# Feed-forward first pass: the stores of normed and transposed rows move from SyncE's queue to ScalarE's

## The reference, cut to what matters

```python
# x: (2, 2048, 1024) float32, N = 4096 rows, D = 1024
x = _layernorm(x + attention(x))            # 32 heads, causal; then out @ wo
# feed-forward, on rows xf = x.reshape(4096, 1024)
h = relu(layernorm(xf @ gw1.T + gb1) * ln_gamma + ln_beta)   # 32 wide
gates = h @ gw2.T + gb2                                       # 8 experts, top 2
counts = onehot.sum(axis=0); allowed = counts <= capacity     # over ALL rows
main = xf @ weight.T
tmp  = einsum('ni,eir->enr', xf, lora_A) * w.T[:, :, None]
out  = main + einsum('enr,ero->no', tmp, lora_B) / 16
x = _layernorm(x + out)
```

## Time and profile before

| | |
|---|---|
| median of 3 runs | 3506.47 us (3506.14 to 3508.07) |
| the profiled execution | 3506.97 us, of which the span is 3505.2 us |
| PE busy | 3426.8 us, 98% of the span |
| DVE / ACT / POOL busy | 2013.6 / 1459.9 / 1743.8 us (57% / 42% / 50%) |
| DMA queues for data | one (q1), 247904 packets, 336.87 MB, 32.2% of 16 engines' span |
| stretch of the first pass | about 2600 to 3110 us |

### The profile page before, as it was taken

The page is one execution under the profiler, slowest core; times in us unless marked ns, Lnnn a source line. Parts: engine busy times, 40 slices in busy tenths (PEclk is TensorE's granted clock), DMA queues, the critical chain, the costliest instruction groups (busy, mean ns, idle before and its releaser), DMA issues.

```text
span 3505.2 us, 61763 instructions
## 1 busy us (share of the span) xinstructions
PE 3426.8 (98%) x25202; PEld 2411.1 (69%) x25202; DVE 2013.6 (57%) x3618; ACT 1459.9 (42%) x1830; POOL 1743.8 (50%) x747
## 2 busy tenths in 40 slices
PE   8999998999999999999999999999998999999999
PEld 7888885566666666666665666666657888878887
DVE  3122116777777667677777767767655666642222
ACT  3111111555555555555555555555542332221111
POOL 0000002888988988898898898889550000000000
PEclk9999997999999999999999999999999999999999
DMA  6334325111121111112112111110037777654553
GB/s 214 114 123 120 113 90 127 26 51 48 32 54 50 35 42 50 42 34 51 48 32 54 50 31 47 50 38 11 26 106 217 234 234 234 211 201 173 173 173 130
DMA packets 248172, 340.60 MB, mean 97 GB/s; under 512 B 55520, under 2 KB 150240, under 8 KB 247904
## 3 DMA queue, kind: packets, MB, share of 16 engines
q1 hardware_dynamic: 247904, 336.87, 32.2%
HBM read 203.08 MB, written 133.17 MB: 96 GB/s over the span
## 4 chain that ended last, share of the span: by engine, by line
PE 78%; DVE 2%; ACT 2%; DMA 1%; issue 1%; POOL 0%; SPq 0%; ACTq 0%; POOLq 0%; DVEq 0%
PE p_o L682 19%; PE p_qm L647 17%; PE p_km L675 12%; PE p_acc L42 7%; PE p_acc L44 7%; PE p_acc L43 7%; PE p_km L668 3%; PE p_qm L651 2%; PE p_km L670 2%; ACT p_probs L759 2%; DVE p_part_max L795 1%; PE p_ag_ps L1096 1%; PE p_acc L1085 1%; DMA p_recip<-reciprocals 1%; PE p_ag_ps L1097 1%
## 5 line engine op out<-in xcount | busy, mean ns | idle before, releaser
L795 DVE TENSOR_REDUCE p_part_max<-p_qm 128x1 f32<-128x512 f32 (+3 forms) x2240 | 1407.0, 670 | 579.5 <-PE p_qm L647 328.8
L618 POOL TENSOR_TENSOR p_psums<-p_psums,p_probs 128x1024 f32<-128x1024 f32 x620 | 1479.3, 2386 | 93.3 <-ACT p_probs L755 2.8
L759 ACT ACTIVATE p_probs<-p_km 128x1024 f32<-128x1024 f32 x896 | 878.5, 1021 | 481.0 <-PE p_km L675 430.8
L647 PE MATMUL p_qm<-p_k_st,p_q_st 96*128 96x512 f32 (+3 forms) x2560 | 913.8, 421 | 12.4 <-DMA p_q_st<-q_hi 10.8
L647 PEld LDWEIGHTS p_qm<-p_k_st,p_q_st 96*128 96x128 f32 x2560 | 481.8, 195 | 254.2 <-issue 112.9
L675 PE MATMUL p_km<-p_q_st,p_k_st 97*128 97x512 f32 x1792 | 599.9, 417 | 13.5 <-ACT p_probs L759 8.7
L682 PE MATMUL p_o<-p_probs,p_v 128*32 128x256 f32 (+1 forms) x9216 | 565.5, 372 | 0.0
L682 PEld LDWEIGHTS p_o<-p_probs,p_v 128*32 128x32 f32 x9216 | 271.5, 110 | 216.7 <-issue 45.2
L675 PEld LDWEIGHTS p_km<-p_q_st,p_k_st 97*128 97x128 f32 x1792 | 312.1, 192 | 112.6 <-ACT p_probs L759 74.7
L614 POOL TENSOR_TENSOR p_psums<-p_probs 128x1024 f32<-128x1024 f32 x110 | 262.1, 2383 | 223.9 <-ACT p_probs L759 223.9
L33 POOL MEMSET p_ident<- 128x128 f32 x2 | 0.4, 204 | 551.0 <-POOLq L64 543.2
(11 more groups left out here) (153 smaller groups left out, 4004.0 us busy)
## 6 DMA issues: line engine op xcount, KB each, us to landing
p_q_st<-q_hi SPq DMA_DIRECT2D x128, 256.0 KB, 4.6
p_x_raw<-in_xT SPq DMA_DIRECT2D x64, 256.0 KB, 3.4
q_hi<-p_out_hi SPq DMA_DIRECT2D x64, 256.0 KB, 2.0
q_lo<-p_out_lo SPq DMA_DIRECT2D x64, 256.0 KB, 2.3
p_q_st<-q_lo SPq DMA_DIRECT2D x64, 256.0 KB, 4.3
attended_T<-p_o_raw SPq DMA_DIRECT2D x128, 128.0 KB
p_a_raw<-attended_T SPq DMA_DIRECT2D x32, 512.0 KB, 4.3
p_recip<-reciprocals SPq DMA_DIRECT2D x128, 128.0 KB, 6.6
```

Source lines behind the costliest of these rows:

```text
L618: pool.tensor_tensor(sums[:, :, :], sums[:, :, :], probs[(n * NS + s) % PB][:, :, :], ALU.add).then_inc(added, 1)
L647: last = pe.matmul(bank[:, x * keys:(x + 1) * keys], q_st[par][0:ROWS, c, h + x, sub * P:(sub + 1) * P], k_st[par][0:ROWS, j * CK:j * CK + ...
L759: act.activation(tile[:, :, :].rearrange("p h q -> p (h q)"), km[s % 2][:, :, :].rearrange("p a b -> p (a b)"), ACT.Exp, scale=SCALE).then ...
L795: dve.reduce_max(part_max[c][:, h:h + heads, sub, j], qm[bank_of(i)][:, 0:item_width(i)].rearrange("p (h k) -> p h k", h=heads), AX.X).the ...
```

## The change

The six lines that issue the three stores leave SP's step and become two functions on ACT, called at the end of ACT's step behind `split_a` and `hidden_root`, ahead of the weight's split. Every wait that stood ahead of a store on SP now stands ahead of it on ACT; SP's own waits for its loads are the same as before.

```diff
@@ sync @@
                     sp.wait_ge(sum_done, t)
                     load_x(t + 1)
-                if 2 <= t < NT + 2:
-                    u = t - 2
-                    sp.wait_ge(yT_lo_done, u + 1)
-                    sp.dma_start(yTh_d[u, :, :, :], yT_hi[:, :, :].bitcast(F32)).then_inc(yT_stored, 16)
-                    sp.dma_start(yTl_d[u, :, :, :], yT_lo[:, :, :].bitcast(F32)).then_inc(yT_stored, 16)
-                if 1 <= t <= NT:
-                    u = t - 1
-                    sp.wait_ge(y_done, u + 1)
-                    sp.dma_start(y_t[u, :, :], y[u % 2][:, :]).then_inc(y_stored[u % 2], 16)
                 if t + 2 < NT:
                     sp.wait_ge(a_lo_done, t + 2)
                     load_a(t + 2)
@@ scalar @@
+            def store_yT(u):
+                act.wait_ge(yT_lo_done, u + 1)
+                act.dma_start(yTh_d[u, :, :, :], yT_hi[:, :, :].bitcast(F32)).then_inc(yT_stored, 16)
+                act.dma_start(yTl_d[u, :, :, :], yT_lo[:, :, :].bitcast(F32)).then_inc(yT_stored, 16)
+
+            def store_y(u):
+                act.wait_ge(y_done, u + 1)
+                act.dma_start(y_t[u, :, :], y[u % 2][:, :]).then_inc(y_stored[u % 2], 16)
+
             def step(t):
@@ step @@
                 if 3 <= t < NT + 3:
                     hidden_root(t - 3)
+                if 2 <= t < NT + 2:
+                    store_yT(t - 2)
+                if 1 <= t <= NT:
+                    store_y(t - 1)
                 for n in range(KC):
                     if t == wm_step(n):
                         split_wm(n)
```

## The result

The changed kernel takes **3520.66 us**, median of 7 runs (3516.85 to 3522.46), against 3506.47 for the kernel before in 7 runs of its own (3505.66 to 3508.07). The ratio is 1.0038, interval 1.0027 to 1.0050: **14 us slower**. 3545.6 had been forecast. The profiled execution took 3519.35 us, with a span of 3517.6, 12.4 above the span before (3505.2).

The account below looks back on a forecast made before the run. PE's 14.6 us round bounds the kernel, the `a_raw` loop within 0.2 us of it. A 12.5 us load plus 3.6 makes 16.1 us; over 27 intervals +38.6 us on 3506.97 gives 3545.6 us, own range 3529 to 3581.

Parts of the forecast that it names:

- what binds: Steady first pass: PE fully busy at 14.6 us per round, the loop through `a_raw` at 14.4 us.
- T: The issue of a load of `a_raw`, at the end of `a_lo`; 3014.95 us in the step read.
- the assumed moment: Stores issued by ACT behind `hidden_root`, at T - 1.1, T - 0.7 and T - 0.3.
- The estimate by work: Load of `a_raw`: 4.0 us of store data less 1.1 us of lead adds 2.9 to 9.1, giving 12.0 us.
- the formula: Time added over the first pass's load loop: 27 P - 396.1, P the load interval; zero at 14.67 us.
- The size of the load at a given lead: Load of `a_raw` with the stores issued from T - 1.1: taken as 12.5 us, range 11.9 to 13.8.
- The base of 9.1 us: Length of the `a_raw` load before the change, read from load 28, issue to landing of the fourth reciprocal load.
- The estimate by landings: Load of `a_raw`: straight line between loads 7 and 4 by when `y` lands, giving 14.0 us.
- ACT's wait for `yT_stored` should stay away: Ahead of `yT_hi` on ACT: the second transposed store has 8.1 us to land, so the wait costs nothing.
- PE's waits of 1 to 2 us in most rounds: Expected sign at the hidden transpose on PE: waits of 1 to 2 us in most rounds.
- No change: Rival: stores fill half-idle DMA engines under the reciprocals, load stays under 11.1 us, 3507 us; chance 0.23.
- Faster: Rival at start-up: load 4 lands in 10.8 us or less, removing PE's stall, 7.7 us, 3499 us; chance 0.12.

Follow-up runs that it names:

- experiment 1: Changed kernel with the three stores still on ACT but ahead of `split_a` and `hidden_root`: 3504.56 us, ratio 0.9989 to the kernel before.
- experiment 4: Changed kernel with a second pair of `a_raw`/`recip` buffers for the odd tiles 3 to 21: 3501.40 us, ratio 0.9980 to the kernel before.
- experiment 5: Changed kernel with ACT waiting for the end of its own `split_a` before issuing the stores: 3554.38 us, ratio 1.0127 to the kernel before.
- experiment 3: Changed kernel with a second pair of `yT_hi`/`yT_lo` buffers for the odd tiles 3 to 19: 3522.03 us, ratio 1.0041 to the kernel before.
- experiment 9: Kernel before, stores on SP held back by a wait for `divide_a` to the moment the changed kernel issues them: 3518.59 us, ratio 1.0033.
- 7: Changed kernel with the edits of experiment 1 and experiment 4 together: 3500.77 us, ratio 0.9979 to the kernel before.
- six kernels of the table: Kernels before and after, experiment 1, experiment 5, experiment 9, and the kernel before with stores on SP behind the wait for `a_lo` (ratio 1.0215).

## Why the prediction was right and wrong

**Right: what binds.** PE had no slack in the steady part, and the loop through `a_raw` lay within 0.2 us of its round. Slower by over 0.2% had chance 0.65, and 3520.66 lies in 3504 to 3578, but below the forecast's own range (3529 to 3581). Experiment 1, which moves only the stores, takes the loss away, and so does experiment 4, which opens the loop.

**Wrong: "In the changed kernel ACT issues the stores behind `hidden_root`, which ends at 3013.87".** The order of the program says so, the chip does not. ACT's queue issued the stores at the start of `split_a` (2849.44 and 2849.44), not at its end. What fits the rows is that a DMA goes out as soon as the waits ahead of it have been passed: in experiment 1 the first store goes out with the start of the ACTIVATE ahead of it (2842.13 for both), and the `y` store, which waits for `y_done`, at that ACTIVATE's end (2843.40). The first store went out at T - 2.3 instead of T - 1.1, and that is the step that failed: with the assumed moment made nearly true (experiment 5, T - 1.25) the kernel is 46 us slower than before (3554.38 against 3508.27), without it 14; 39 had been forecast. The estimate by work, 9.1 + 4.0 less the lead, gives 10.8 us at T - 2.3, where 11.5 was measured. Had I put the right lead into the same sum and taken the same half microsecond more, 11.3 us, the formula would have given +6.

**The size of the load at a given lead** was nearly right, 12.5 taken and 12.8 measured, but partly by luck, since two errors cancel. The base of 9.1 us is load 28, the shortest of 27; their mean is 10.5. And the stores add less than was taken: 3.4 us in the prediction, 2.9 by its estimate by work, but 2.4 measured at T - 1.25 (12.9 against 10.5) and 0.9 at T - 2.3. The same short base made the loop look as if it had 1.9 us of room (12.7 against 14.6); with the mean load it is 14.1, with 0.5 us. The estimate by landings (14.0) was not right. Load 4 blended two troubles, as the text suspected, and the time at which `y` lands is a poor measure: in experiment 1 the `y` store issued at 2843.4 took 7.7 us, to 2851.1, 3.2 us behind the load's issue, and the load was not slowed. When a store lands does not tell when it is out of the load's way.

**Wrong: "ACT's wait for `yT_stored` should stay away".** It became 72.8 us in 25 steps. The reckoning had 8.1 us for the store to land, because `yT_hi` starts at T + 7.4. But that distance is not a constant: once the load, and no longer PE, sets the round, PE's last matmuls of the round end with `a_lo`, and `yT_hi` is ready soon behind T. The "about 1 us on either side" of the data had no row behind it either. In the step above the store issued at 2849.80 lands 3.8 us later and lets `yT_hi` start at T + 1.9. The price put on it, nothing, was right: experiment 3 takes two thirds of it away and gains nothing, since `divide_a` waits until T + 11 for the load anyway.

**PE's waits of 1 to 2 us in most rounds**: seen in 13 rounds, at 7.1 us in all, the longest 1.3. It fits a loop only 0.5 us longer than PE's round. DVE's wait for the reciprocals, over 100 us in about 27 steps, was right (105.0 in 28). So was the share of the DMA engines in a load's first 5 us, "near 1"; behind it the share falls to 0.62 at 128 GB/s, not as far as the 0.45 and 79 GB/s of the earlier trace rows. In the 3.6 us before the load it is 0.48, where "near 0.3" stood, since the stores move there already:

```profile
2848.18:2851.78 3.60, 3.55 (x27) 3.20 (x25) 2.47 (x3) 1.90 (x3) 0.00 (x0) 1.00 0.48 190
2851.00:2855.00 4.00, 2.69 (x15) 2.19 (x15) 3.69 (x15) 2.40 (x4) 0.00 (x0) 1.00 1.01 310
2855.00:2857.00 2.00, 2.00 (x11) 1.65 (x10) 1.97 (x3) 0.01 (x1) 0.00 (x0) 1.00 1.07 312
2857.00:2862.00 5.00, 5.00 (x24) 3.87 (x23) 3.19 (x10) 1.54 (x2) 0.00 (x0) 1.00 0.62 128
```

**No change** (0.23) was nearer in time than the forecast, by 14 us against 25, but for none of its reasons: the stores did not hide in the idle share, they went out earlier than assumed. Its condition, a load under 11.1 us, was missed by 0.4. The rule of the Trainium skill that stood beside it ("DMA: Bandwidth & Descriptors", section "Issuing engines are not separate DMA queues") agrees with experiment 9 against the change: the same moment on one queue or on two costs the same. The 3507 us that followed from it was off by 14, because here the change of issuer also changed the moment: with the same three DMAs on ACT's queue the ratio goes from 0.9989 to 1.0127 by the moment alone (experiments 1 and 5).

**Faster** (0.12) did not come, since load 4 gained too little: 14.8 us (2651.21 to 2666.01) instead of 16.5, as the stores were still issued only 2.3 us ahead of it. Its mechanism is real: in experiment 1 load 4 takes 10.1 us (2645.66 to 2655.75), and no stall of PE at the hidden rows there exceeds 1.7 us. In that one execution, the fastest of eleven, the span is 9.3 us shorter than before; in the median the whole is worth 0.1%, about 4 us, less than the 7.7 us reckoned.

**The best version** is a second `a_raw` with the stores on ACT (experiment 4, or 7): 3501.4 against 3508.77, 0.2% below before.

## What to carry to other kernels

Where a loop through a single buffer lies within a few per cent of the bounding engine's round, the question for any transfer is not which queue issues it but at which moment of the loop its data moves. Look for the gap in which the critical load is not in flight, and compare the issue time with the release of that load to a tenth of a microsecond, since here a delay of 1.1 us cost 32 to 35 us of kernel (experiment 5 against the change). Take the length of a transfer as the mean of all its instances and not from one step. A new wait of 73 us beside it may cost nothing: ask what the waiting instruction is late for, and open the loop with a second buffer before tuning the order in it.

## What was not expected of the hardware

- A DMA on ACT's queue was issued while the ACTIVATE ahead of it in the program had only started: 2849.44 for both, and the same in all 27 steps; in experiment 5, with a wait on that ACTIVATE's end, 1.09 us after its start (2829.88 to 2830.97).
- The load was slowed in its issues, not in its landing. With the stores 4.5 us or more ahead, the fourth reciprocal load was issued 2.1 to 2.3 us behind the load's first issue; with them 2.3 us ahead it was 3.2, at 1.7 it was 4.0 and at 1.25 it was 4.5, though in the changed kernel and in experiment 5 the stores stood in the other queue. Its landing took 8.2 to 8.5 us from its issue in all six kernels of the table. I read it as an issue that waits while the DMA engines are full; no run tested that by itself.
- In the changed kernel load and stores run from two queues. The Trainium skill ("DMA: Bandwidth & Descriptors", section "Queues, rings and completion order") says that an engine alternates between them by packets. The times do not show the alternation, since one queue in experiment 9 gave 15.10 us and two gave 15.06.
